# Attention with two half-array heads: where TensorE turns the values of the item before, and which engine divides them by their sums

## The chip, the cores and the metric

The kernel runs on one core of one Trainium2 chip. The metric is the device time of one execution in microseconds, the smaller the better. The core's engines are TensorE (PE in the profile, with its weight loads as PEld), VectorE (DVE), ScalarE (ACT), GpSimd (POOL) and SyncE (SP, which here only issues DMAs). They run their own instruction streams and meet at semaphores.

## The reference

The program is a sandwich of two layers over 4 x 2048 tokens of 256 channels: a recurrent scan, a routed feed-forward stage, a first attention with rotary embedding, and a second one with grouped projections. The change touches the first attention alone:

```python
# 16 heads of 16 channels; the batch is 4, the sequence is 2048 here
q = _apply_rope(xq, cos, sin)
k = _apply_rope(xk, cos, sin)
scores = jnp.einsum('bqhd,bkhd->bhqk', q, k) / jnp.sqrt(jnp.asarray(HEAD_DIM, dtype=q.dtype))
attn = jax.nn.softmax(scores, axis=-1)
out = jnp.einsum('bhqk,bkhd->bqhd', attn, xv)
```

## The kernel before

`phase_attention` (from L239) is called twice. With 16 channels a head (`DH = 16`) its flag `TWO` is true, and there are `N = 64` items, one for each pair of batch and head. With 32 channels a head `TWO` is false, and none of the touched code is used in that call.

An item is worked through in a window of `NSB = 64` steps. Every engine has its own list of what it does at each step, written out in Python (`window(n, s)`), unrolled for 12 items, then a loop of three rounds of 12 items, then the last 16 unrolled. What follows is the order within one window.

- **Scores and exponentials.** At each step TensorE makes one tile of 128 keys by 512 queries (`scores`, L550, tile `S`, written `at_S` in the profile). The contraction has 48 rows of split queries and keys and two rows with the running maximum, so 50 rows. At even steps it stands in rows 0 to 49 of the array, at odd steps in rows 64 to 113 (`HALVES`). ScalarE takes the exponential into `PB` (`exps`, L630). The tiles `S` are a ring of `NSR = 3` PSUM banks.
- **Maxima of the item after.** At each even step TensorE also makes two tiles of 512 scores (`max_scores`, L521, tile `MX`, 48 rows), one in rows 0 to 47 and one in rows 64 to 111. VectorE takes the negated maximum of both (`maxima`, L684). `MX` is a ring of two, so the matmuls of step t wait for the reduction of step t - 4. After 32 reductions a small one (L689) and a transpose (L540, step 50) give the rows of maxima of the next item; GpSimd splits them in two (`m_parts`, L456 and L458).
- **Values.** At each even step four products of 128 keys with a part of 256 queries (`values`, L561, tile `AV`) add up the numerators and, in one column, the sum. They are in fp32, so the profile counts eight matmuls. They use the full 128 rows and 32 of the array's columns each.
- **Turning.** The values of item n - 1 are complete after step 4 of window n. ScalarE copies `AV` to `AVS` after the exponential of step 4 (`put_values`, L638). TensorE turns `AVS` with four fp32 transposes of 128 x 128 (`turn_values`, L580) into a bank of the ring `S`. ScalarE copies this to `FO` (`take_values`, L648). Then VectorE takes the reciprocal of the 16 sums of each partition (`invert_turned`, L695), GpSimd multiplies (`normalise_turned`, L466) into `O`, and SyncE stores `O`.

`OUT_STEP` is 7. Before the change TensorE's order around it is: `MX` and `S` of step 6, the values of step 6 (the first of item n, which wait until `AVS` is copied), the four transposes, `S` of step 7, `MX` and `S` of step 8, the values of step 8. The list `places(n)` gives the ring `S` its order of occupants. ScalarE does `take_values` ahead of the exponential of step 7. VectorE and GpSimd do their parts at step 11.

Of the kernel before, what the change touches and what calls it, by code (L numbers as in the profile page):

```python
# [7 lines left out]
ALU = mybir.AluOpType  # L8
# [230 lines left out]
def phase_attention(nc, tag, H, DH, scale, qk_d, v_d, out_d, ident_d):  # L239
# [61 lines left out]
    def places(n):  # L301

        out = []
        for t in range(NSB):
            if TWO and t == OUT_STEP and (not isinstance(n, int) or n > 0):
                out.append(("out", 0))
            out.append(("score", t))
            if t == TURN_AT and later(n, 1):
                out.append(("turn", 0))
        return out  # L310
# [20 lines left out]
    with ExitStack() as ctx:  # L331
# [109 lines left out]
        @block.gpsimd  # L441
        def _(pool):
            for u in range(NBUF):
                for h in HALVES:
                    lo = (h + NQ) // 32 * 32
                    ins = nc.gpsimd.memset(KT[u][lo:lo + 32, :].bitcast(F32), 1.0)
                ins.then_inc(preset, 1)
            if not TWO:
                pool.wait_ge(preset, NBUF)
                nc.gpsimd.memset(ONES[:, :], 1.0).then_inc(preset, 1)  # L450

            def m_parts(it):

                wait(pool, mrow, 32 * len(HALVES) * it)
                wait(pool, nmf_got, it + 1, pool_step)
                nc.gpsimd.tensor_copy(NMR[:, 0, :], NMF[:, :]).then_inc(nmr_split, 1)  # L456
                wait(pool, nmr_split, it + 1)
                nc.gpsimd.tensor_tensor(NMR[:, 1, :], NMF[:, :], NMR[:, 0, :].bitcast(F32),  # L458
                                        ALU.subtract).then_inc(nmr_ready, 1)

            def normalise_turned(it, s):
                fo = FO[s % 2][:, :].rearrange("p (j c d) -> p j c d", j=W // P, c=NCH)
                out = O[s % 2][:, :, :].rearrange("p (c j) d -> p j c d", c=NCH)
                wait(pool, ostored[s % 2], 8 * NSTORE * it - 8 * NSTORE * (s % 2), pool_step)
                wait(pool, rec_done, it + 1, pool_step)
                nc.gpsimd.tensor_tensor(out, fo[:, :, :, 0:DH],  # L466
                                        REC[s % 2][:, :, :].to_broadcast([P, W // P, NCH, DH]),
                                        ALU.mult).then_inc(norm_done, 1)

            def add(it, i, kb):  # L470

                first = GROUPS[i][0]
                k = NCH * kb % NPB
                total = SUM[(len(GROUPS) * it + i) % 2]
                wait(pool, exp_done, NSB * it + NCH * (kb + 1))
                if kb == first + 1:
                    k0 = NCH * first % NPB
                    wait(pool, l_done, len(GROUPS) * it + i - 1)
                    other = PB[:, k0:k0 + NCH, :]
                else:  # L480
                    wait(pool, sum_done, NADD * it + added(kb) - 1)
                    other = total[:, :, :]
                nc.gpsimd.tensor_tensor(total[:, :, :], other, PB[:, k:k + NCH, :], ALU.add).then_inc(sum_done, 1)  # L483

            m_parts(0)

            def adds(n, s, t):
                for i, (a, b) in enumerate(GROUPS):
                    for kb in range(a + 1, b):
                        if NCH * (kb + 1) == t:  # L490
                            add(n, i, kb)

            def window(n, s):
                for t in range(NSB):
                    for unit in running(n, s, t):
                        adds(*unit)
                    if TWO and t == OUT_STEP + 4 and (not isinstance(n, int) or n > 0):
                        normalise_turned(n - 1, s + NBUF - 1)
                    if t == TURN_AT and later(n, 1):
                        m_parts(n + 1)  # L500
            rounds(pool, window)
            if TWO:
                normalise_turned(N - 1, N - 1)
            for t in range(NSB, 2 * NSB):
                adds(N - 1, N - 1, t)

        @block.tensor
        def _(pe):
# [90 lines left out]
            def window(n, s):  # L599

                for t in range(NSB):
                    tile = tile_at(t)
                    if TWO and t == OUT_STEP and (not isinstance(n, int) or n > 0):
                        slot_free(n, "out")
                        turn_values(n - 1, s + NBUF - 1, item(n, s, "out")[1])
                    if tile and later(n, tile[0]):
                        max_scores(n + tile[0], s + tile[0], tile[1])
                    scores(n, s, t)
                    for unit in running(n, s, t):
                        outputs(*unit)  # L610
                    if t == TURN_AT and later(n, 1):
                        slot_free(n, "turn")
                        max_turn(n + 1, item(n, s, "turn")[1])
# [7 lines left out]
        @block.scalar  # L621
        def _(act):
            def exps(it, s, t):
                old, of = (t - NPB, it) if t >= NPB else (t + (NSB - 1 - t) // NPB * NPB, it - 1)
                wait(act, av_done, NBLK * of + old // NCH + 1)
                if not TWO:
                    wait(act, sum_done, NADD * of + added(old // NCH))
                i, r = item(it, s, "score", t)
                wait(act, s_put, i + 1)
                nc.scalar.activation(PB[:, t % NPB, :], SP_[r][:, :],  # L630
                                     ACT.Exp, scale=scale).then_inc(exp_done, 1)

            def put_values(it, s):

                if not TWO:
                    wait(act, norm_done, it - 1)
                wait(act, av_done, NBLK * (it + 1))
                nc.scalar.activation(AVS[s % 2][:, :], AV[:, :], ACT.Copy).then_inc(avs_ready, 1)  # L638

            def take_turned(it, i, r):  # L640
                wait(act, nmr_ready, it)
                wait(act, s_put, i + 1)
                nc.scalar.activation(NMF[:, :], SP_[r][0:NBLK, 0:P], ACT.Copy).then_inc(nmf_got, 1)  # L643

            def take_values(it, s, i, r):
                wait(act, norm_done, it - 1)
                wait(act, s_put, i + 1)
                nc.scalar.activation(FO[s % 2][:, :], SP_[r][:, :], ACT.Copy).then_inc(fo_got, 1)  # L648

            def put_sums(it):  # L650

                wait(act, rec_done, NCH * it)
                wait(act, l_done, len(GROUPS) * (it + 1))
                nc.scalar.activation(LS[:, :], L[:, :], ACT.Copy).then_inc(ls_ready, 1)  # L654

            def window(n, s):
                for t in range(NSB):
                    if TWO and t == OUT_STEP and (not isinstance(n, int) or n > 0):
                        take_values(n - 1, s + NBUF - 1, *item(n, s, "out"))
                    exps(n, s, t)  # L660
                    for it, s_, t_ in running(n, s, t):
                        if END_STEP == t_:
                            put_values(it, s_)
                        if not TWO and sum_step(len(GROUPS) - 1) + 1 == t_:
                            put_sums(it)
                    if t == TURN_AT and later(n, 1):
                        take_turned(n + 1, *item(n, s, "turn"))
            take_turned(0, 0, 0)
            rounds(act, window)
            put_values(N - 1, N - 1)  # L670
            if TWO:
                take_values(N - 1, N - 1, TAIL, TAIL % NSR)
            else:
                put_sums(N - 1)

        @block.vector
        def _(dve):
# [10 lines left out]
                    wait(dve, nmf_got, it)  # L688
                    nc.vector.tensor_reduce(NM[:, :], NM4[:, :, :], AX_X, ALU.min).then_inc(nm_ready, 1)  # L689

            def invert_turned(it, s):
                fo = FO[s % 2][:, :].rearrange("p (j c d) -> p j c d", j=W // P, c=NCH)
                wait(dve, norm_done, it - 1)
                wait(dve, fo_got, it + 1)
                nc.vector.reciprocal(REC[s % 2][:, :, :], fo[:, :, :, DH]).then_inc(rec_done, 1)  # L695

            def invert(it, s, q):

# [25 lines left out]
            def window(n, s):  # L724
                for t in range(NSB):
# [4 lines left out]
                        for unit in running(n, s, t):  # L730
                            outputs(*unit)
                    if TWO and t == OUT_STEP + 4 and (not isinstance(n, int) or n > 0):
                        invert_turned(n - 1, s + NBUF - 1)
            rounds(dve, window)
            if TWO:
                invert_turned(N - 1, N - 1)
            else:
                for t in range(NSB, 2 * NSB):
                    outputs(N - 1, N - 1, t)
# [1172 lines left out]
```

## Time and profile before

| | us |
|---|---|
| median of 3 runs | 6774.84 |
| the three runs | 6770.58, 6774.84, 6792.63 |
| the profiled execution: its own time | 6770.58 |
| its span, first to last instruction | 6768.8 |
| the first attention, roughly | 1657 to 4340 of the span |

The profile is of one execution. "Busy" is time in which an engine had an instruction in work; the ends of matmuls are modelled, so their starts are what to read. An idle time is put down to what ended it. A row of the chronological view merges neighbours of a kind: "x4" are four instructions.

### The profile page before, as it was taken

What the parts mean: (1) busy time and instruction counts of PE and PEld (TensorE: products, weight loads), DVE (VectorE), ACT (ScalarE), POOL (GpSimd) and SP (SyncE); (2) the same over time, 40 slices, a digit from 0 to 9 for tenths busy, and PEclk for the clock granted to TensorE, in tenths of its full rate; (3) what the DMA queues carried; (4) which work ended last, traced back from release to release, by engine and by line L of the source; (5) the groups of instructions that cost most, each with busy time, mean ns of one, the idle gap of its engine ahead of it and who ended that gap; (6) DMA issues with size and microseconds to landing.
All of it is one profiled execution on the core that took longest, in us unless ns stands there. A gap on an engine that the chain in (4) does not pass through costs nothing. (4 is left out here: it accounts for less than half of the span.)

```text
span 6768.8 us, 116415 instructions
## 1 busy us (share of the span) xinstructions
PE 5861.4 (87%) x39184; PEld 2627.0 (39%) x39184; DVE 5338.4 (79%) x7223; ACT 4001.9 (59%) x7095; POOL 2223.9 (33%) x1114
## 2 busy tenths in 40 slices
PE   5996766675999999999999999756999999999992
PEld 3443541442333333333333333333444444444432
DVE  6996510775999999999999999587878787888855
ACT  3773101110788888888888888611556666666660
POOL 2332100343000000000000000011789888888891
PEclk9998866776999999999999999865999999999995
DMA  4112566455333333333333333286111111111106
GB/s 140 50 47 95 175 245 227 133 175 139 48 49 49 52 54 47 53 52 50 49 49 49 49 53 46 66 242 182 37 38 38 37 38 38 38 32 35 39 6 202
DMA packets 373239, 548.75 MB, mean 81 GB/s; under 512 B 68464, under 2 KB 273200, under 8 KB 352976
## 3 DMA queue, kind: packets, MB, share of 16 engines
q1 hardware_dynamic: 359888, 524.77, 32.1%
q10 hardware_dynamic: 12800, 16.78, 0.7%
q8 instruction: 328, 5.37, 0.3%
q14 instruction: 223, 1.83, 0.1%
HBM read 352.02 MB, written 186.78 MB: 80 GB/s over the span
## 5 line engine op out<-in xcount | busy, mean ns | idle before, releaser
L684 DVE TENSOR_REDUCE at_NM<-at_MX 128x1 f32<-128x1024 f32 (+1 forms) x4096 | 3750.4, 950 | 550.7 <-PE at_MX L521 517.3
L630 ACT ACTIVATE at_PB<-at_S 128x512 f32<-128x512 f32 x6144 | 3308.1, 599 | 977.0 <-PE at_S L550 859.7
L521 PE MATMUL at_MX<-at_KT,at_QT 48*128 48x512 f32 (+1 forms) x6144 | 2408.3, 454 | 169.5 <-DVE at_NM L684 91.0
L550 PE MATMUL at_S<-at_QT,at_KT 50*128 50x512 f32 (+1 forms) x6144 | 2339.1, 435 | 6.7 <-ACT at_PB L630 3.8
L561 PE MATMUL at_AV<-at_PB,at_VS 128*32 128x256 f32 (+1 forms) x20480 | 1821.4, 437 | 18.5 <-ACT at_AVS L638 13.2
L550 PEld LDWEIGHTS at_S<-at_QT,at_KT 50*128 50x128 f32 (+1 forms) x6144 | 1009.9, 188 | 904.0 <-issue 477.8
L521 PEld LDWEIGHTS at_MX<-at_KT,at_QT 48*128 48x128 f32 (+1 forms) x6144 | 996.7, 190 | 738.4 <-DVE at_NM L684 555.7
L483 POOL TENSOR_TENSOR at_SUM<-at_SUM,at_PB 128x2048 f32<-128x2048 f32 x192 | 885.2, 4610 | 60.8 <-ACT at_PB L630 44.7
L561 PEld LDWEIGHTS at_AV<-at_PB,at_VS 128*32 128x32 f32 x20480 | 431.5, 108 | 1018.6 <-ACT at_PB L630 784.6
L483 POOL TENSOR_TENSOR at_SUM<-at_PB 128x2048 f32<-128x2048 f32 x160 | 749.9, 4688 | 148.8 <-ACT at_PB L630 148.3
L456 POOL CAST at_NMR<-at_NMF 16x128 fp32r<-16x128 f32 x96 | 26.9, 280 | 1630.3 <-ACT at_NMF L643 1630.3
L1354 ACT ACTIVATE r_XT<-r_PT 128x1024 f32<-128x1024 f32 x48 | 49.2, 1024 | 569.8 <-PE r_PT L1263 569.8
L466 POOL TENSOR_TENSOR at_O<-at_FO,at_REC 128x256 f32<-128x256 f32 x64 | 39.8, 622 | 1027.0 <-DVE at_REC L695 1027.0
L833 PE MATMUL wkv_PQ<-wkv_XT,wkv_WT 128*128 128x512 f32 x768 | 339.2, 598 | 42.6 <-DVE wkv_DL L953 25.8
L833 PEld LDWEIGHTS wkv_PQ<-wkv_XT,wkv_WT 128*128 128x128 f32 x768 | 144.1, 191 | 237.3 <-issue 192.9
L1204 POOL TENSOR_SCALAR r_veps<-r_mv 128x4 f32<-128x4 f32 x112 | 25.7, 229 | 601.9 <-DVE r_mv L1414 601.9
L912 POOL TENSOR_TENSOR wkv_EV<-wkv_E2S,wkv_V 128x1024 f32<-128x1024 f32 x32 | 75.6, 2362 | 355.0 <-DVE wkv_MN L931 152.9
L1250 PE MATMUL r_PA<-r_OW,r_A 128*128 128x256 f32 x512 | 137.0, 434 | 62.9 <-DVE r_X L1478 47.8
L572 PE MATMUL at_L<-at_SUM,at_ONES 128*32 128x512 f32 x1280 | 177.3, 627 | 8.0 <-POOL at_SUM L483 8.0
L703 DVE RECIPROCAL at_REC<-at_LS 128x128 f32<-128x128 f32 x128 | 119.8, 940 | 71.9 <-ACT at_LS L654 71.9
L1283 PE MATMUL r_QK<-r_WQ,r_XT 128*128 128x512 f32 x256 | 153.4, 732 | 19.8 <-ACT r_XT L1354 19.8
L1434 DVE TENSOR_TENSOR r_RT<-r_QK,r_ROPE 128x256 f32<-128x256 f32 x256 | 90.2, 414 | 89.8 <-PE r_QK L1283 87.0
(153 smaller groups left out, 4181.1 us busy)
## 6 DMA issues: line engine op xcount, KB each, us to landing
moe_W<-in_w SPq DMA_DIRECT2D x64, 1024.0 KB, 10.8
at_QT<-qk SPq DMA_DIRECT2D x384, 128.0 KB, 5.9
at_KT<-qk SPq DMA_DIRECT2D x384, 128.0 KB, 7.3
qk<-r_HI SPq DMA_DIRECT2D x64, 512.0 KB, 4.1
qk<-r_LO SPq DMA_DIRECT2D x64, 512.0 KB, 4.7
x<-r_X SPq DMA_DIRECT2D x48, 512.0 KB, 3.0
at_VS<-v SPq DMA_DIRECT2D x96, 256.0 KB, 8.5
at_QT<-qk SPq DMA_DIRECT2D x96, 256.0 KB, 4.1
```

Source lines behind the costliest of these rows:

```text
L483: nc.gpsimd.tensor_tensor(total[:, :, :], other, PB[:, k:k + NCH, :], ALU.add).then_inc(sum_done, 1)
L521: ins = nc.tensor.matmul(MX[r][:, a, :], QT[u][h:h + NQ, b * P:(b + 1) * P], KT[u][h:h + NQ, (c + a) * W:(c + a + 1) * W], start=True, sto ...
L550: nc.tensor.matmul(SP_[item(it, s, "score", t)[1]][:, :], KT[u][h:h + NQ + 2, kb * P:(kb + 1) * P], QT[u][h:h + NQ + 2, c * W:(c + 1) * W] ...
L561: ins = nc.tensor.matmul(AV[c * VW:(c + 1) * VW, cols], VS[s % NBUF][:, kb, :], PB[:, (NCH * kb + c) % NPB, cols], start=first, stop=last)
L572: ins = nc.tensor.matmul(L[c * VW:(c + 1) * VW, :], ONES[:, :], SUM[(len(GROUPS) * it + i) % 2][:, c, :], start=(i == 0), stop=(i == len(G ...
L630: nc.scalar.activation(PB[:, t % NPB, :], SP_[r][:, :], ACT.Exp, scale=scale).then_inc(exp_done, 1)
L684: nc.vector.tensor_reduce(NM4[:, b, c:c + 1], MX[r][:, :, :].rearrange("p a n -> p (a n)"), AX_X, ALU.max, negate=True).then_inc(ring_got, 1)
L703: nc.vector.reciprocal(REC[s % 2][:, part], LS[:, part]).then_inc(rec_done, 1)
L833: ins = nc.tensor.matmul(PQ[q][:, tt * 512:(tt + 1) * 512], WT[:, cc, row:row + P], XT[b % 2][:, cc, t0:t0 + 512], start=(cc == 0), stop=( ...
L1250: ins = nc.tensor.matmul(PA[:, j, :], A[u][:, q, t], OW[:, q, :], start=(q == 0), stop=(q == 2 * CC - 1))
L1283: ins = nc.tensor.matmul(QK[j % 2][:, :], XT[u][:, c, t], WQ[:, c, 0:2 * D], start=(c == 0), stop=(c == CC - 1))
L1434: ins = nc.vector.tensor_tensor(RT[k][:, :, :, :], qk[:, :, :, :, r], cs[f][:, :, :, :], ALU.mult)
```

## The change

Two things are done together, both only for `TWO`.

1. In step 7 the turning comes behind the score tile, on TensorE (the score matmul is issued first and then the four transposes), on ScalarE (the exponential first, then the copy to `FO`) and in the list of places of the ring.
2. GpSimd's `normalise_turned` is taken out. VectorE's `invert_turned` becomes `normalise_turned`: it takes the reciprocal, waits for its own result (`rec_done`) and for the earlier store of `O` (`ostored`), and multiplies itself. Its old wait for `norm_done` goes.

```diff
         for t in range(NSB):
+            out.append(("score", t))
             if TWO and t == OUT_STEP and (not isinstance(n, int) or n > 0):
                 out.append(("out", 0))
-            out.append(("score", t))
...
-            def normalise_turned(it, s):
-                fo = FO[s % 2][:, :].rearrange("p (j c d) -> p j c d", j=W // P, c=NCH)
-                out = O[s % 2][:, :, :].rearrange("p (c j) d -> p j c d", c=NCH)
-                wait(pool, ostored[s % 2], 8 * NSTORE * it - 8 * NSTORE * (s % 2), pool_step)
-                wait(pool, rec_done, it + 1, pool_step)
-                nc.gpsimd.tensor_tensor(out, fo[:, :, :, 0:DH],
-                                        REC[s % 2][:, :, :].to_broadcast([P, W // P, NCH, DH]),
-                                        ALU.mult).then_inc(norm_done, 1)
-
...
                     tile = tile_at(t)
-                    if TWO and t == OUT_STEP and (not isinstance(n, int) or n > 0):
-                        slot_free(n, "out")
-                        turn_values(n - 1, s + NBUF - 1, item(n, s, "out")[1])
                     if tile and later(n, tile[0]):
                         max_scores(n + tile[0], s + tile[0], tile[1])
                     scores(n, s, t)
                     for unit in running(n, s, t):
                         outputs(*unit)
+                    if TWO and t == OUT_STEP and (not isinstance(n, int) or n > 0):
+                        slot_free(n, "out")
+                        turn_values(n - 1, s + NBUF - 1, item(n, s, "out")[1])
...
-                    if TWO and t == OUT_STEP and (not isinstance(n, int) or n > 0):
-                        take_values(n - 1, s + NBUF - 1, *item(n, s, "out"))
                     exps(n, s, t)
...
+                    if TWO and t == OUT_STEP and (not isinstance(n, int) or n > 0):
+                        take_values(n - 1, s + NBUF - 1, *item(n, s, "out"))
...
-            def invert_turned(it, s):
+            def normalise_turned(it, s):
                 fo = FO[s % 2][:, :].rearrange("p (j c d) -> p j c d", j=W // P, c=NCH)
-                wait(dve, norm_done, it - 1)
+                out = O[s % 2][:, :, :].rearrange("p (c j) d -> p j c d", c=NCH)
                 wait(dve, fo_got, it + 1)
                 nc.vector.reciprocal(REC[s % 2][:, :, :], fo[:, :, :, DH]).then_inc(rec_done, 1)
+                wait(dve, rec_done, it + 1)
+                wait(dve, ostored[s % 2], 8 * NSTORE * it - 8 * NSTORE * (s % 2))
+                nc.vector.tensor_tensor(out, fo[:, :, :, 0:DH],
+                                        REC[s % 2][:, :, :].to_broadcast([P, W // P, NCH, DH]),
+                                        ALU.mult).then_inc(norm_done, 1)
```

## Rows read from the trace of the kernel before

**Rows 1.** The page, the span in 40 equal slices: busy tenths, granted TensorE clock.

```profile
PE   5996766675999999999999999756999999999992
DVE  6996510775999999999999999587878787888855
ACT  3773101110788888888888888611556666666660
PEclk9998866776999999999999999865999999999995
```

**Rows 2.** Two stretches of 400 us inside the first attention, busy time by engine.

```profile
1800.00:2200.00 400.00, 397.60 (x3818) 149.98 (x3814) 384.47 (x334) 350.99 (x657) 12.87 (x29) 1.00 0.33 49
3400.00:3800.00 400.00, 397.69 (x3816) 150.15 (x3809) 383.31 (x334) 351.17 (x657) 12.76 (x28) 1.00 0.35 52
```

**Rows 3.** ScalarE's copy to FO, between 2900 and 3100 us.

```profile
L648 ACT ACTIVATE at_FO<-at_S x5: 598/598/598, 2906.8 to 3069.9; 128x512 f32<-128x512 f32 x5
```

**Rows 4.** Who TensorE waited for between 1800 and 4300 us.

```profile
PE at_AV L561 <- ACT at_AVS L638: 12.2, 58, 0.5
PE at_MX L521 <- issue: 6.3, 4, 2.9
PE at_AV L561 <- issue: 5.2, 2, 2.9
```

**Rows 5.** TensorE in order of time, steps 5 to 8 of one window.

```profile
2904.65 0.50 PE L550 MATMUL at_S<-at_QT,at_KT 50*128 50x512 f32 x1
2904.66 0.73 PE L521 MATMUL at_MX<-at_KT,at_QT 48*128 48x512 f32 x2
2905.00 0.40 PE L550 MATMUL at_S<-at_QT,at_KT 50*128 50x512 f32 x1
2905.58 0.64 PE L561 MATMUL at_AV<-at_PB,at_VS 128*32 128x256 f32 x8 [0.18 <-ACT at_AVS L638]
2906.15 0.66 PE L580 MATMUL at_S<-at_ident,at_AVS 128*128 128x128 f32 x4
2906.73 0.49 PE L550 MATMUL at_S<-at_QT,at_KT 50*128 50x512 f32 x1
2906.74 0.72 PE L521 MATMUL at_MX<-at_KT,at_QT 48*128 48x512 f32 x2
2907.07 0.40 PE L550 MATMUL at_S<-at_QT,at_KT 50*128 50x512 f32 x1
2907.40 0.64 PE L561 MATMUL at_AV<-at_PB,at_VS 128*32 128x256 f32 x8
```

**Rows 6.** TensorE at the last item, where no MX matmuls are left.

```profile
4333.05 0.50 PE L550 MATMUL at_S<-at_QT,at_KT 50*128 50x512 f32 x1
4333.48 0.42 PE L561 MATMUL at_AV<-at_PB,at_VS 128*32 128x256 f32 x4
```

**Rows 7.** TensorE in the second attention, matmuls of one kind in a row.

```profile
5501.82 0.40 PE L550 MATMUL at_S<-at_QT,at_KT 98*128 98x512 f32 x1
5502.06 0.40 PE L521 MATMUL at_MX<-at_KT,at_QT 96*128 96x512 f32 x1
```

**Rows 8.** ScalarE in order of time, steps 5 to 12 of the same window as rows 5.

```profile
2906.84 0.60 ACT L648 ACTIVATE at_FO<-at_S 128x512 f32<-128x512 f32 x1 [0.34 <-PE at_S L580]
2907.33 3.49 ACT L630 ACTIVATE at_PB<-at_S 128x512 f32<-128x512 f32 x6
```

**Rows 9.** VectorE in order of time, the same window, and TensorE's MX of step 16.

```profile
2909.88 0.25 DVE L695 RECIPROCAL at_REC<-at_FO 128x16 f32<-128x16 f32 x1
2910.04 1.16 DVE L684 TENSOR_REDUCE at_NM<-at_MX 128x1 f32<-128x1024 f32 x1
2911.69 0.50 PE L521 MATMUL at_MX<-at_KT,at_QT 48*128 48x512 f32 x1
```

**Rows 10.** Start of the phase, where MX waits for VectorE, in order of time.

```profile
1656.95 2.35 DVE L684 TENSOR_REDUCE at_NM<-at_MX 128x1 f32<-128x1024 f32 x2 [53.56 <-PE at_MX L521]
1659.36 0.80 PE L521 MATMUL at_MX<-at_KT,at_QT 48*128 48x512 f32 x2 [0.33 <-DVE at_NM L684]
```

**Rows 11.** VectorE in order of time, later in the same window.

```profile
2927.34 1.23 DVE L684 TENSOR_REDUCE at_NM<-at_MX 128x1 f32<-128x1024 f32 x1
2928.60 0.19 DVE L689 TENSOR_REDUCE at_NM<-at_NM 128x16 f32<-128x32 f32 x1
2928.91 5.86 DVE L684 TENSOR_REDUCE at_NM<-at_MX 128x1 f32<-128x1024 f32 x5
```

**Rows 12.** Multiplications on VectorE: one line each, shortest/median/longest in ns.

```profile
L1434 DVE TENSOR_TENSOR r_RT<-r_QK,r_ROPE x256: 389/414/426, 1212.9 to 1600.7; 128x256 f32<-128x256 f32 x128
L709 DVE TENSOR_TENSOR at_O<-at_AVS,at_REC x32: 691/3854/4160, 4830.5 to 6612.6; 128x512 f32<-128x512 f32 x32
```

**Rows 13.** The end of the first attention, in order of time.

```profile
4337.60 0.26 DVE L695 RECIPROCAL at_REC<-at_FO 128x16 f32<-128x16 f32 x1 [34.81 <-ACT at_FO L648]
4338.00 0.62 POOL L466 TENSOR_TENSOR at_O<-at_FO,at_REC 128x256 f32<-128x256 f32 x1 [34.44 <-DVE at_REC L695]
```

More of the change, by code:

```diff
@@ L496, in window @@
                         adds(*unit)
-                    if TWO and t == OUT_STEP + 4 and (not isinstance(n, int) or n > 0):
-                        normalise_turned(n - 1, s + NBUF - 1)
                     if t == TURN_AT and later(n, 1):
@@ L501, in _ @@
             rounds(pool, window)
-            if TWO:
-                normalise_turned(N - 1, N - 1)
             for t in range(NSB, 2 * NSB):
@@ L732, in window @@
                     if TWO and t == OUT_STEP + 4 and (not isinstance(n, int) or n > 0):
-                        invert_turned(n - 1, s + NBUF - 1)
+                        normalise_turned(n - 1, s + NBUF - 1)
             rounds(dve, window)
             if TWO:
-                invert_turned(N - 1, N - 1)
+                normalise_turned(N - 1, N - 1)
             else:
```

## The prediction

> **What bounds the kernel now.** I read the slices first [rows 1]: the first attention is the long stretch (about 1657 to 4340 us) in which TensorE and VectorE both stand at 9 and ScalarE at 8, with the clock at full speed. Busy shares can't say which of the two sets the pace (TensorE 398 of 400 us, VectorE 384 [rows 2]), so I went on to the waits. TensorE has three entries between 1800 and 4300 us [rows 4]: its values waiting for the copy to AVS (12.2 us in 58 windows, 0.2 each), and two for "issue". It never waits for VectorE's reductions nor for an exponential. An engine that waits for nobody sets the pace. One window takes (3069.9 - 2906.8) / 4 = 40.8 us [rows 3].
>
> Then the starts on TensorE, around the turning [rows 5]. Two steps are a packet: S and MX start together (2904.65, 2904.66), then MX and S (2905.00), then the eight of AV. From the four transposes on, the distances are: transposes to the next packet 0.58, first pair to second pair 0.34, second pair to AV 0.33, and AV to AV over the whole piece 1.82, of which 1.24 are a normal packet (0.34 + 0.33, and 0.57 for AV: 2906.15 - 2905.58). So the turning costs 0.58 us of TensorE's time, and whatever is added to TensorE here is added to the window.
>
> **The change on TensorE.** Nothing is added to the list, only an order is changed: S of step 7 goes ahead of the transposes. But S of step 7 loses its partner. Before, S(7) stood in the rows from 64 on and the first MX in rows 0 to 47, and they started together; then the second MX (64 on) and S(8) (0 on). After it, S(7) runs alone between AV and the transposes, the two MX start together, and S(8) stands alone behind them. Three rounds instead of two.
>
> What the additional round costs: at the last item there is an S all alone, cold, with a matmul of another kind behind it: 4333.05 to 4333.48, 0.43 us [rows 6]. It is the same situation (S first after AV, then a matmul that uses the array otherwise). The rest keeps its distances: AV to S(7) as AV to the transposes before, transposes to the MX pair 0.58, MX pair to S(8) 0.34, S(8) to AV 0.33 [rows 5]. New path less old path: (0.43 + 0.58 + 0.34 + 0.33) - (0.58 + 0.34 + 0.33) = **0.43 us for each window**. From below it is bounded by 0.24 us, the distance at which full-height matmuls of one kind follow each other with their weights loaded ahead [rows 7]; and by 0, if TensorE had slack after all. From above I take 0.53: the MX pair is now cold (0.50 long against 0.40 for a second one [rows 5]), if S(8) pays for that as well. I take 0.43, since the row is the very pair of neighbours.
>
> The Trainium skill (TensorEngine Tiling (Array Packing), Key Properties) says that a change of tiling mode, not of tile, drains the array. The order before has two changes between AV and S(7); the new one has three up to MX. The trace agrees that such a border costs something: 0.33 from a second pair to AV against 0.24 within one kind [rows 5, 7]. By the border alone, 0.09 us a window, the sum below would be 62 x 0.09 = 6 us.
>
> Windows 1 to 63 turn a value. The last has no MX and waits for its exponentials, so 62 count: 62 x 0.43 = **+26.7 us**.
>
> **ScalarE.** It is idle 0.34 us ahead of the copy to FO [rows 8], as it waits for the transposes with nothing to do. With S(7) first it has an exponential for this time. The idle goes, and is worth nothing: behind the copy come six exponentials without a gap in 3.49 us, ScalarE catches up, and TensorE waits for none of them [rows 4]. The wait for AVS stays too, since both orders have the values of step 6 ahead. New in the ring: S(10) now follows FO. The copy ends some 0.43 us later than now, at 2906.84 + 0.60 = 2907.44 [rows 8], and S(10) starts 0.57 + 0.34 behind the AV of 2907.40, at 2908.31 [rows 5], and also comes 0.43 later, which leaves some 0.8 us. No price.
>
> **VectorE.** It gets the multiplication, 128 x 256. Nearest row: 414 ns at that shape [rows 12]. L709 has both inputs in SBUF as this one: 691 ns at 512 columns at its shortest, so 414 at 256 fits; the upper bound is that 691. L709's median of 3854 ns is under GpSimd's long additions in the second attention; in the first, GpSimd works 13 us in 400 [rows 2], and nothing at step 11.
>
> The Trainium skill (SBUF — State Buffer, Who interferes with whom) says a VectorE instruction with two SBUF inputs and a GpSimd one that reads SBUF block each other. The trace agrees by that spread of 691 to 4160 ns; a lock of this sort would cost 3 us a window, and has no partner here.
>
> Does it reach TensorE? VectorE has time over: behind the small reduction it runs five large ones at (5.86 - 1.22) / 4 = 1.16 us [rows 11] where a packet gives it 1.24. But the ring of two MX is short. The reduction of step 12 ends at 2910.04 + 1.16 = 2911.20, and MX(16) starts at 2911.69, 0.49 later [rows 9]. Where MX does wait for VectorE, it starts 0.06 behind the reduction's end (1656.95 + 2.35 = 1659.30, then 1659.36) [rows 10]. So VectorE may come 0.43 us later than now. After the change, behind the reciprocal come 0.25 for its end, a wait for its own result (0.03 to 0.04, as the small reduction starts behind the large one's end, 2928.57 [rows 11]; up to 0.15, as GpSimd takes 0.14 with the same two waits [rows 13]), 0.41 for the multiplication, less 0.08 of overlap: the reduction starts 0.62 to 0.73 behind the reciprocal's start, not 0.16 [rows 9]. That is 0.46 to 0.57 later, against 0.43 to spare. TensorE stalls 0.03 to 0.14 us; I take 0.07, nearer the lower end, as it is VectorE's own row (up to 0.35 with a multiplication of 691 ns; 0 from below), once, since VectorE gains 0.08 on each further packet. 62 x 0.07 = **+4.3 us**. What hides the remaining 0.4 us is the slack of the ring; without it the multiplication would cost 62 x 0.5 = 31 us.
>
> **GpSimd and SyncE.** GpSimd loses 622 ns a window of work nobody waited for; its maxima at step 50 come at the same time. `norm_done` comes earlier, so the store does. Only at the end of the phase it counts: reciprocal to end of product is 1.02 us now [rows 13], and 0.25 + 0.04 + 0.41 = 0.70 after: -0.3 us, once.
>
> **Sum.** +26.7 + 4.3 - 0.3 = +30.7 us. On the profiled execution's own 6770.6 us that is 6801; the median of the runs is 4.3 us higher, 6775, which gives 6806. I give 6804, +0.45%.
>
> **The rivals.** A measurement of this kernel can't tell less than about 0.3%, 20 us, from no change.
>
> *The product is dear.* At 691 ns or with slow waits the stall is 0.35 us a window: 62 x 0.35 = 22 in place of 4, in all 6822. For it speaks the odd access pattern (a broadcast input, an output in another order), against it that no row in this kernel shows a pattern to matter.
>
> *The lone S is cheap.* It costs only the border between kinds (0.09) or the bare stream of its columns (0.24 [rows 7]): 6 to 15 us over 62 windows; with 2 us of stall 6779 to 6788 on the own time. For it: 0.43 holds 0.10 of weight load, which might overlap the AV before. Against: S after AV always shows 0.50.
>
> *Nothing on the path.* If VectorE or ScalarE had set the pace all along, the lone S would be hidden: 6771 to 6777. Against it, TensorE's empty list of waits.
>
> *Faster: ScalarE's gap was the path.* If the stream of exponentials decides the window, the 0.34 us ahead of FO fall out: 62 x 0.34 = 21 us, 6751. For it: ScalarE idles there in every window. It decides from the point where a score tile or value waits for an exponential at steps 8 to 12, and none does.
>
> **How the numbers follow.** Forecast 0.56 (6793 to 6813 by itself), dear product 0.14, cheap S 0.13, nothing 0.09, faster 0.08. Leaving out the faster case and the dearest end gives a range of 6776 to 6819. Slower by over 0.3%: the forecast less its lowest end, and the dear product, 0.66. Within 0.3%: 0.26. Faster: 0.08.
>
> **What would show it.** In the profile after: copies to FO 41.3 us apart, not 40.8. On TensorE after AV(6) an S alone, transposes 0.43 later, two MX starting together, an S 0.34 behind. AV(6) to AV(8) 2.25 us, not 1.82. On ScalarE no idle ahead of FO. On VectorE the product 0.41 long, some 0.04 to 0.15 behind the reciprocal, and the reduction 0.6 to 0.7 behind its start. A first wait of MX for a reduction on TensorE's list, near step 16, under 0.15 us each. It is wrong if the transposes follow S(7) in 0.25 or less, or if TensorE's gap at step 16 is above 0.3.

## The result: 0.7% slower, beyond the range

| | median us | runs |
|---|---|---|
| before | 6774.84 | 5 (6770.58 to 6792.63) |
| changed | 6836.81 | 5 (6822.44 to 6839.26) |
| ratio over all runs of the comparison | 1.007 | 95% interval 1.0057 to 1.0083 |

I had forecast 6804 with a range of 6776 to 6819 and slower at 0.66. The direction held, the size did not: +62 us between the first medians, where I had +31 to the own time. Those two medians are an unlucky pair, one below and the other above the mean of its kernel. Over 17 runs the changed kernel took 6828.7 us in the mean, and the kernel before 6780.6 over 5 here and 6782 to 6787 in three later comparisons (19 to 24 runs each). The first comparison gives +48 us, a later one +45, and all runs on record together (22 and 71) +45. I go on with **+47 us**, of which my steps give two thirds.

The profiled execution took 6836.09 us (span 6834.3). The slices of the page that answer to [rows 1]:

```profile
PE   5996766775999999999999999765999999999993
DVE  6996510775999998998999999587878788878855
ACT  3773101111888888888888888611466666656660
PEclk9998866776999999999999999865899999999995
```

Inside the first attention nothing is to be seen at this grain but an 8 twice in VectorE's row, where it had only 9. The two places matter later.

ScalarE's copy to FO, unrolled windows first, then windows of the loop (answer to [rows 3]; before it was 40.8 in both):

```profile
L635 ACT ACTIVATE at_FO<-at_S x4: 597/598/598, 1929.4 to 2053.4; 128x512 f32<-128x512 f32 x4
...
L635 ACT ACTIVATE at_FO<-at_S x4: 597/597/597, 2982.7 to 3106.8; 128x512 f32<-128x512 f32 x4
```

That is 124.0 / 3 = 41.33 and 124.1 / 3 = 41.37 us a window. TensorE in order of time at steps 6 to 8 of a loop window, the answer to [rows 5]:

```profile
2980.98 0.64 PE L548 MATMUL at_AV<-at_PB,at_VS 128*32 128x256 f32 x8 [0.18 <-ACT at_AVS L625]
2981.55 0.50 PE L537 MATMUL at_S<-at_QT,at_KT 50*128 50x512 f32 x1
2981.98 0.66 PE L567 MATMUL at_S<-at_ident,at_AVS 128*128 128x128 f32 x4
2982.57 0.50 PE L508 MATMUL at_MX<-at_KT,at_QT 48*128 48x512 f32 x2
2982.91 0.40 PE L537 MATMUL at_S<-at_QT,at_KT 50*128 50x512 f32 x1
2983.23 0.64 PE L548 MATMUL at_AV<-at_PB,at_VS 128*32 128x256 f32 x8
```

S(7) stands alone; the transposes start 0.43 behind it, the two MX together 0.59 further on, S(8) 0.34 behind them, AV 0.32 behind that. AV to AV is 2.25 us, before 1.82.

The lone S pays for a round of its own between two borders, and not for its missing partner as such. In the last windows of the kernel before, two score matmuls in the two halves stand between the transposes and the values, and they take the same 0.43:

```profile
4301.68 0.50 PE L550 MATMUL at_S<-at_QT,at_KT 50*128 50x512 f32 x2
4302.11 0.42 PE L561 MATMUL at_AV<-at_PB,at_VS 128*32 128x256 f32 x4
```

VectorE in order of time in the same window, and TensorE at step 16 (answer to [rows 9]):

```profile
2985.71 0.24 DVE L682 RECIPROCAL at_REC<-at_FO 128x16 f32<-128x16 f32 x1
2986.08 0.43 DVE L685 TENSOR_TENSOR at_O<-at_FO,at_REC 128x256 f32<-128x256 f32 x1
2986.42 2.35 DVE L671 TENSOR_REDUCE at_NM<-at_MX 128x1 f32<-128x1024 f32 x2
...
2987.52 0.50 PE L537 MATMUL at_S<-at_QT,at_KT 50*128 50x512 f32 x1
2987.70 0.56 PE L508 MATMUL at_MX<-at_KT,at_QT 48*128 48x512 f32 x2
```

The same places in an unrolled window:

```profile
2015.02 0.24 DVE L682 RECIPROCAL at_REC<-at_FO 128x16 f32<-128x16 f32 x1
2015.30 0.43 DVE L685 TENSOR_TENSOR at_O<-at_FO,at_REC 128x256 f32<-128x256 f32 x1
2015.64 1.22 DVE L671 TENSOR_REDUCE at_NM<-at_MX 128x1 f32<-128x1024 f32 x1
...
2016.84 0.50 PE L537 MATMUL at_S<-at_QT,at_KT 50*128 50x512 f32 x1
2016.91 0.66 PE L508 MATMUL at_MX<-at_KT,at_QT 48*128 48x512 f32 x2
```

S and MX of step 16 used to start together. Now MX comes 0.18 later in the loop (0.16 of it reach the window) and 0.07 later unrolled, since the product starts 0.13 behind the end of the reciprocal in the loop (2985.95 to 2986.08) and 0.04 behind it unrolled. In the unrolled code the values it waits for are constants, in the loop they depend on the round; that this makes the difference is likely, and was not tested. In the unrolled window MX starts 0.05 behind the end of the reduction (2016.86), the same distance as in [rows 10], so it is the reduction that it waits for, although TensorE's list of waits has no entry of that name. The two stalls and the lone S are the whole change in an ordinary window: 0.43 + 0.07 = 0.50 and 0.43 + 0.16 = 0.59. Over 26 unrolled and 36 loop windows that is 34.2 us; with the 0.60 by which the loop's windows differ over the whole trace it is 34.6. I go on with **34.5 us**. Some 12 of the 47 us are not in ordinary windows.

They are in the first attention all the same. From the first copy to FO to the last it takes 2582.4 us before and 2634.5 after, 52 more; in the second traces of the two kernels, taken later, it takes 2586.1 and 2630.6, 44 more. So 10 to 18 us of the phase are beyond its windows:

```profile
L648 ACT ACTIVATE at_FO<-at_S x64: 597/598/600, 1754.5 to 4336.9; 128x512 f32<-128x512 f32 x64
L635 ACT ACTIVATE at_FO<-at_S x64: 592/597/598, 1763.8 to 4398.3; 128x512 f32<-128x512 f32 x64
```

These are behind the loop's back edges, the two places where the loop jumps back to its head. Two stretches of each trace, around the first and the second back edge; the columns are as in [rows 2] (busy time of TensorE, its weight loads, VectorE, ScalarE and GpSimd, then the granted clock, the DMA share and GB/s). Before, and after:

```profile
2690.00:2790.00 100.00, 95.70 (x881) 35.94 (x881) 87.88 (x77) 81.02 (x152) 3.31 (x7) 0.95 0.35 51
3180.00:3290.00 110.00, 104.55 (x964) 39.16 (x964) 96.53 (x85) 89.09 (x167) 3.32 (x7) 0.95 0.34 50
```

```profile
2690.00:2790.00 100.00, 94.64 (x756) 34.52 (x754) 76.36 (x69) 70.18 (x130) 1.45 (x4) 0.81 0.28 42
3180.00:3290.00 110.00, 103.90 (x864) 38.20 (x863) 87.66 (x78) 80.52 (x150) 1.45 (x4) 0.86 0.27 41
```

The clock has two levels, 2.4 and 1.2 GHz, so a mean of 0.95 over 100 us are 10 us at the lower one, and 0.81 are 38. At each back edge TensorE stands still twice for some 3 us, and from the second stop on the clock is at half. The first back edge of the kernel before, and behind it the values of a packet every 2.16 us:

```profile
2691.08 0.51 PE L521 MATMUL at_MX<-at_KT,at_QT 48*128 48x512 f32 x2 [2.92 <-issue]
2694.74 1.08 PE L561 MATMUL at_AV<-at_PB,at_VS 128*32 128x256 f32 x8 [2.86 <-issue]
2696.89 1.08 PE L561 MATMUL at_AV<-at_PB,at_VS 128*32 128x256 f32 x8
2699.05 1.08 PE L561 MATMUL at_AV<-at_PB,at_VS 128*32 128x256 f32 x8
```

The stops are the second and third line of [rows 4], which the prediction left out of its sum. In the kernel before the clock stayed at half for 10 and 11 us, in the changed one for 38 and 31. TensorE stays "busy" in both, at half the pace (756 matmul records in place of 881), so busy time doesn't show it. The Trainium skill (Runtime: NRT & Kernel Launch, Instruction fetch mechanics) says that a taken branch can force a fetch of instructions by DMA before execution goes on. The trace agrees with that: the stops stand at the loop's back edges, and nowhere in the phase when it is written out, and in the 10 us around the two stops (2685 to 2695) nine packets of the kind "instruction" land, where 40 us of straight code (2720 to 2760) have seven.

```profile
q8 instruction: 3, 0.05, 2.4%
q14 instruction: 6, 0.05, 1.6%
```

### The profile page after: what moved, and what is told of

The parts are those of the page before. It is cut to its first block and busy times, and to the rows that moved or that the text cites. A ratio compares the mean times of both kernels' runs of the same rounds, so it can differ in the third digit from the quotient of the medians.

```text
span 6834.3 us, 116275 instructions
## 1 busy us (share of the span) xinstructions
PE 5932.6 (87%) x39184; PEld 2657.6 (39%) x39184; DVE 5352.9 (78%) x7287; ACT 4013.1 (59%) x7095; POOL 2186.3 (32%) x1050
## 3 DMA queue, kind: packets, MB, share of 16 engines
q14 instruction: 222, 1.82, 0.1%
## 5 line engine op out<-in xcount | busy, mean ns | idle before, releaser
L537 PE MATMUL at_S<-at_QT,at_KT 50*128 50x512 f32 (+1 forms) x6144 | 2369.2, 437 | 6.7 <-ACT at_PB L617 3.7
L537 PEld LDWEIGHTS at_S<-at_QT,at_KT 50*128 50x128 f32 (+1 forms) x6144 | 1024.1, 189 | 930.7 <-issue 506.6
L1242 PEld LDWEIGHTS r_PA<-r_OW,r_A 128*128 128x128 f32 x512 | 112.5, 223 | 95.2 <-issue 68.7
```

Of the source, the lines that this page charges most:

```text
L537: nc.tensor.matmul(SP_[item(it, s, "score", t)[1]][:, :], KT[u][h:h + NQ + 2, kb * P:(kb + 1) * P], QT[u][h:h + NQ + 2, c * W:(c + 1) * W] ...
L1242: ins = nc.tensor.matmul(PA[:, j, :], A[u][:, q, t], OW[:, q, :], start=(q == 0), stop=(q == 2 * CC - 1))
```

## The experiments

Three theories on the 12 us: the order makes the half-clock stretches longer (A), the product on VectorE does (B), their length is chance and the same in both kernels (C).

**Part 1 alone** (the order of places, of TensorE and of ScalarE, without the product; of its edit only the list of places is shown):

```diff
+            out.append(("score", t))
             if TWO and t == OUT_STEP and (not isinstance(n, int) or n > 0):
                 out.append(("out", 0))
-            out.append(("score", t))
...
```

> Part 1 alone: the turning behind the score of step 7, the product stays on GpSimd. Both theories: TensorE pays 0.43 us a window for the lone score matmul, windows of 41.2 us in place of 40.8, +27 us over 62. They differ on the half-clock stretches behind the two back edges of the loop, which were 10 us long each before and 38 and 31 us after. Theory A (the order makes them long): again some 30 us or more, about +20 us on top, +45 in all. Theory B (the product on VectorE makes them long): 10 us, +27 in all. Theory C (their length is set by where the back edge falls in time, whatever the kernel): anything between, and the kernel before shows long ones too in some executions.

Measured: 1.0064 (1.0041 to 1.0087), +39 us in the mean of 4 runs (error 7), where its windows give 27. ScalarE's copy to FO in the loop:

```profile
L648 ACT ACTIVATE at_FO<-at_S x6: 597/597/597, 2920.5 to 3126.4; 128x512 f32<-128x512 f32 x6
```

205.9 / 5 = 41.18 us, 0.42 above before. By the granted clock (0.95 of 100 us, 0.83 of 110) the stretches were 10 and 37 us: one as before, one long.

**Part 2 alone** (the product on VectorE, the old order; GpSimd's multiplication is gone as in the change):

```diff
+                wait(dve, rec_done, it + 1)
+                wait(dve, ostored[s % 2], 8 * NSTORE * it - 8 * NSTORE * (s % 2))
+                nc.vector.tensor_tensor(out, fo[:, :, :, 0:DH],
+                                        REC[s % 2][:, :, :].to_broadcast([P, W // P, NCH, DH]),
+                                        ALU.mult).then_inc(norm_done, 1)
```

> Part 2 alone: the product on VectorE, the turning ahead of the score of step 7 as before. MX of step 16 waits for VectorE: 0.07 us in an unrolled window, 0.16 in a window of the loop, 27 x 0.07 + 35 x 0.16 = +7.5 us; no lone score, so the pairs stay. Theory A: the half-clock stretches stay at 10 us, +7.5 in all. Theory B: they are 30 us or more, +27. Theory C: either.

Measured: 1.0016 (1.0004 to 1.0028), +9 us in the mean of 10 runs, where its windows give 7.5. Stretches of 18 and 11 us (0.91 and 0.95). Theory B's +27 did not come. The two parts, +0.64% and +0.16%, add up to 0.80%, and both together took 0.70% and 0.71%; the intervals cover the difference.

**The kernel before once more.**

> The kernel before, unchanged, once more with a profile: windows of 40.8 us. Theories A and B: half-clock stretches of 10 us behind the back edges and 6771 to 6775 us. Theory C: in some executions 20 to 40 us and 6790 us, as two of the five timed runs of before.

6775.4 us, one run. The same two stretches of the trace:

```profile
2690.00:2790.00 100.00, 94.74 (x817) 34.88 (x817) 82.11 (x72) 75.60 (x141) 2.69 (x6) 0.88 0.28 42
3180.00:3290.00 110.00, 104.36 (x975) 39.07 (x973) 97.36 (x86) 89.93 (x170) 3.42 (x8) 0.97 0.28 43
```

24 and 7 us: the length is not a constant of the kernel. The trace that I predicted from had two short ones.

**The turning behind the score of step 8**, product on GpSimd. It tests the account of pairs and borders: this place is no earlier than the changed one, but breaks no pair and adds no border. The reciprocal and the product stay at step 11.

```diff
-    OUT_STEP = END_STEP + 3 - NSB
+    OUT_STEP = END_STEP + 4 - NSB
...
                     scores(n, s, t)
+                    if TWO and t == OUT_STEP and (not isinstance(n, int) or n > 0):
+                        slot_free(n, "out")
+                        turn_values(n - 1, s + NBUF - 1, item(n, s, "out")[1])
                     for unit in running(n, s, t):
                         outputs(*unit)
```

> The turning behind the score of step 8 and ahead of the values of step 8, so that no pair of score and MX is broken and there is no further border between kinds; the product stays on GpSimd. By the account of pairs and borders it costs TensorE nothing: windows of 40.8 us, +0 us. If it was the later turning itself that cost (a bank of the ring of scores that comes free later, a later copy to FO), it costs as much as part 1 or more: 41.2 us and +27. Theory A, taken as the broken pair: stretches of 10 us.

Measured: 0.9986 (0.9973 to 0.9999). TensorE in order of time:

```profile
2952.24 0.49 PE L550 MATMUL at_S<-at_QT,at_KT 50*128 50x512 f32 x1
2952.24 0.72 PE L521 MATMUL at_MX<-at_KT,at_QT 48*128 48x512 f32 x2
2952.58 0.40 PE L550 MATMUL at_S<-at_QT,at_KT 50*128 50x512 f32 x1
2952.90 0.66 PE L580 MATMUL at_S<-at_ident,at_AVS 128*128 128x128 f32 x4
2953.49 0.64 PE L561 MATMUL at_AV<-at_PB,at_VS 128*32 128x256 f32 x8
```

The pairs are whole, S to the transposes is 0.32 (not 0.43), the transposes to AV 0.59, and the window does not grow. What cost in the change is the round that the lone S has to itself, not the later turning. The missing partner and the additional border come together in part 1, and no run parts them. Stretches of 10 and 13 us.

**Part 1 only at the head of each round** (windows 12, 24, 36), **and everywhere but there.** A function of the place in the code picks the order; in the loop `s` runs from 0 to 11 in every round:

```diff
+    def behind(s):
+        return TWO and (s in (0, 12, 24, 36))
...
-                    if TWO and t == OUT_STEP and (not isinstance(n, int) or n > 0):
+                    if not behind(s) and TWO and t == OUT_STEP and (not isinstance(n, int) or n > 0):
```

> Part 1 only in the windows 12, 24 and 36 (those at the head of a round of the loop; 24 and 36 come behind a back edge), all other windows as before. The lone score matmul costs 3 x 0.43 = 1.3 us. Theory A (a lone score matmul at step 7 behind a back edge keeps the clock down longer): +12 us or more in the mean, stretches of 30 us. Theory C (the length is chance, alike in both kernels): +1 us.

Measured: 1.0009 (0.9997 to 1.0021), +5 us in the mean of 11 runs, stretches of 10 and 31 us. It lies between theory C's +1 and A's +12, with an error of 4, and so decides nothing.

The other kernel has `s not in (0, 1, 48)`:

> Part 1 in all windows but 1, 12, 24, 36 and 48, which keep the old order: 58 or so windows at 0.43 us are +25 us. Theory A: that and no more, since behind the back edges nothing is changed. Theory C: the same +25. If part 1 costs more than its windows wherever it stands: +35.

Since `s` is 1 in the loop too, the windows 13, 25 and 37 kept the old order as well, and 54 windows pay and not 58: 23 us. Measured: 1.0032 (1.0021 to 1.0044), +21 us in the mean of 6 runs. Nothing on top, as A says; stretches of 28 and 18 us. With this one and the last, neither the heads of the rounds alone nor the other windows alone show the 12 us, so they can't be pinned on the windows right behind an edge.

**The changed kernel once more.**

> The changed kernel once more, on the chip of the other three. Its windows cost 27 x 0.50 + 35 x 0.60 = +34.5 us. Theory A: +47 with longer stretches in most executions. Theory C: +35 in the mean over many runs, and the +62 between the first medians was partly luck.

Measured: 1.0071 (1.0058 to 1.0085), +45 us in the mean, with an error of 3. Stretches of 28 and 37 us (0.86 of 100, 0.83 of 110). The first ratio was no accident, and C's +35 is out.

**The turning behind step 8 once more.**

> The turning behind the score of step 8 once more, product on GpSimd, for a narrower interval: unrolled windows of 40.64 us in place of 40.83 and loop windows of 40.74 in place of 40.76, -5 us, so a ratio of 0.9992. The first comparison had 0.9986, a part of which would be chance.

Measured: 1.001 (1.0000 to 1.0021), where the first time it was 0.9986. The two intervals don't meet, so 0.1% between such sets of runs means nothing; with the loop this order is no faster. The two traces of this one kernel differ in their windows too: in the loop 40.75 us here, and there 40.48 and 40.74 in turn. Stretches of 24 and 7 us.

**Rounds of 4 items** (`UNR = 4`), to have 13 back edges in place of 2, for all four combinations.

> The kernel before with rounds of 4 items in place of 12 (UNR = 4), so 13 back edges in place of 2: each costs two stops of TensorE of some 3 us and a half-clock stretch, in all 9.4 us at the 10 us stretches of the first trace, so 11 more of them are +103 us or more, some 6885. It gives 13 stretches for the comparison with the next three. Theory C (length is chance): a mean of about 15 us, as in the five traces without a lone score matmul behind the edge, with single ones of 25 or 30.

> The changed kernel with rounds of 4 items. Against the kernel before with rounds of 4, the windows cost 62 x 0.43 and 56 x 0.16, +36 us. Theory A (lone score matmul behind an edge) or B (product): stretches of some 33 us in the mean in place of 15, 13 x 18 us at half clock, of which some 0.42 is lost, +98 us on top. Theory C: the same lengths as in the kernel before and +36 us.

> Part 1 alone with rounds of 4 items. Windows +27 us against the kernel before with rounds of 4. Theory A: most of the 98 us of longer stretches are here. Theory B: none of them, +27. Theory C: +27.

> Part 2 alone with rounds of 4 items. Windows +9 us against the kernel before with rounds of 4. Theory A: +9 and short stretches. Theory B: the long stretches are here, +100. Theory C: +9.

The stretch from 1900 to 4200 us, in the order before, changed, part 1 alone, part 2 alone:

```profile
1900.00:4200.00 2300.00, 2242.41 (x20481) 836.95 (x20478) 2059.66 (x1790) 1889.91 (x3528) 70.84 (x158) 0.95 0.32 47
```

```profile
1900.00:4200.00 2300.00, 2258.75 (x19897) 845.19 (x19899) 2011.32 (x1790) 1847.00 (x3427) 37.35 (x102) 0.92 0.32 46
```

```profile
1900.00:4200.00 2300.00, 2258.62 (x19969) 838.32 (x19967) 2009.70 (x1746) 1851.43 (x3438) 68.75 (x153) 0.92 0.32 47
```

```profile
1900.00:4200.00 2300.00, 2249.82 (x20385) 845.40 (x20381) 2057.00 (x1835) 1880.57 (x3510) 38.53 (x106) 0.95 0.32 47
```

A clock of 0.95 is 230 us at half clock, 0.92 is 368. It goes with the order, not with the product, so B is out. But the timed runs don't follow: 6949.6, 6989.4, 6982.5 and 6938.4 us in the mean of 5, 4, 4 and 4. Both kernels with the new order together are 42 us above both with the old one; their windows explain 27, so 13 back edges cost 15 us more, with an error of about 8, and not the 98 that I had expected of A. The profiled executions were the fastest of their kernel in the old order (6919.57, 6923.9) and among the slowest in the new (7000.95), so the traces overstate it. Part 2 alone came out 11 us below before, where +9 had been expected; the error of that difference is 9. What these runs do show well: with rounds of 4 a back edge costs (6949.6 - 6782.3) / 11 = 15 us on average, and the 9.4 us in the trace of before was a cheap one.

**The 64 windows written out** (`UNR = N`), so that there is no back edge at all.

> The kernel before with the first attention's 64 windows all written out (no loop, so no back edge). All theories: windows of 40.83 us, no stop of 3 us on TensorE and no half-clock stretch inside the phase. 35 windows at +0.07 are +2 us; two back edges gone are -19 us by the first trace of before, -30 us by the 15 us that each further edge cost in the runs with rounds of 4. So -17 to -28 us, a ratio of 0.996 to 0.9975.

> The changed kernel with the 64 windows written out. Against the one before written out: 62 x 0.50 = +31 us by the windows. Theory A (the part of some 11 us that the windows leave unexplained is in the half-clock stretches behind the back edges): +31 and no more. If it is elsewhere (start of the phase, second attention, ends): +42.

Measured: the kernel before written out 0.9962 (0.995 to 0.9975), mean of 10 runs 6763.2; the changed one written out 1.0007 (0.9997 to 1.0017), mean of 12 runs 6788.3. Windows from 2900 us on, before and changed:

```profile
L648 ACT ACTIVATE at_FO<-at_S x5: 598/598/598, 2924.3 to 3087.6; 128x512 f32<-128x512 f32 x5
```

```profile
L635 ACT ACTIVATE at_FO<-at_S x5: 598/598/598, 2915.4 to 3080.5; 128x512 f32<-128x512 f32 x5
```

163.3 / 4 = 40.83 and 165.1 / 4 = 41.28 us. The second has one short window in it; nearly all others take 41.3, which is the 0.50 more. From the first copy to FO to the last it is 2564.2 and 2595.6 us, 31 more, as the windows say. The only wait left on TensorE in the phase is the one for AVS, the clock is 1.00 throughout, and the difference of the means is 25 us with an error of 3. The 12 us on top are gone with the back edges.

**The clock of the timed runs.** A trace shows one execution, but the mean granted clock of every timed run is on record too. Twice what is missing to 1, times the run's span, is its time at half clock, all phases together. The clock is given to three decimals, 14 us of this time, so only means say something:

| | us at half clock | runs |
|---|---|---|
| before, four comparisons | 1262 (error 3) | 71 |
| changed, two | 1287 (4) | 22 |
| part 1 alone | 1286 (8) | 4 |
| part 2 alone | 1262 (5) | 10 |
| part 1 at the heads alone, everywhere but there | 1269 (8), 1264 (5) | 11, 6 |
| turning behind step 8, first and second time | 1256 (4), 1283 (7) | 10, 12 |
| rounds of 4: old order, new order | 1521 (13), 1594 (14) | 9, 8 |
| written out: before, changed | 1237 (7), 1225 (3) | 10, 12 |

The changed kernel spends 24 us more at half clock, with an error of 5. A packet takes 2.16 us there for 1.24, so 0.43 of this time is lost: 10 us of the 12. Part 1 alone has the same 24, part 2 alone has none, so B is out in the timed runs as well, and C, which has the same lengths in both kernels, does not fit. Written out, the changed kernel has 12 us less at half clock than before and not more, worth 5 us, about as much as 25 falls short of the windows' 31. With rounds of 4 the new order has 73 us more, worth 31 (error 8), where the times left 15 (error 8). Two rows follow no simple rule: part 1 at the heads alone has no clear excess, and the turning behind step 8 has 1283 in its second set without any lone score.

**The turning behind step 8, written out**, the version that beats both.

> The turning behind the score of step 8, product on GpSimd, windows written out: unrolled windows of this order took 40.64 to 40.81 us against 40.83, so -1 to -12 us against the kernel before written out, with nothing from back edges to blur it.

Measured: 0.9954 (0.994 to 0.9968), 6752.65 us median of 6 runs. Of the 0.46%, 0.38% are the missing back edges; against the kernel before written out the means differ by 11 us, with an error of 3.

```profile
L648 ACT ACTIVATE at_FO<-at_S x7: 603/603/605, 2905.6 to 3149.4; 128x512 f32<-128x512 f32 x7
```

243.8 / 6 = 40.63 us a window. Behind the turning a packet takes 1.23 us in place of 1.24 in many windows; why was not tried.

## Why the prediction was right or wrong

- **What sets the pace.** Right. In an ordinary window TensorE waits for nobody but AVS before, and both what the order and what the late MX put on it are in the window.
- **The lone score, 0.43 us.** Right to the hundredth (0.43 in the trace, 0.42 by the windows of part 1 alone), because the row of the last item was the same pair of neighbours. The bounds of 0 and 0.24 were not needed. That the order costs, and not the later turning, is shown by the turning behind step 8: no earlier, no pair broken, no cost.
- **ScalarE's idle time.** Right that removing it is worth nothing. The idle ahead of FO is gone, and the rival that went faster with it.
- **The product on VectorE.** The mechanism right, to the step at which MX first waits. The wait for its own result is 0.04 unrolled and 0.13 in the loop; I had both as ends of a range and took a stall of 0.07 for all windows. Measured are stalls of 0.07 and 0.16, 7.5 us in place of 4.3. The sign that I had named for it, an entry on TensorE's list of waits, did not come; the starts show it. The product takes 0.43 us, not 0.69: the dear product did not come.
- **The sum.** Here it failed. It took the phase for 62 equal windows at full clock. "Issue" had a place in the list of waits [rows 4], 11.5 us, and the prediction put it at nothing and called the list empty: two stops of 3 us at each back edge, followed by a stretch at half clock. The term missing from the sum is the part of the cost that is paid behind the back edges, some 12 us. That it is there is shown by difference: 47 us less 34.5 with the loop, 25 against 31 without it. That most of it is a longer stay at half clock is what the clock of the timed runs says (24 us more, worth 10), and the profiles too. Over the ten traces with two back edges, the stretches with no lone S behind the edge average 15 us (twelve of them, 7 to 28), those with one 28 us (eight, 10 to 38); 13 us more cost 5.5, twice. Part 2 alone doesn't have it.
- **The range.** Its upper end came from one dear instruction. It should have held what varies from run to run: medians of before lie between 6774.8 and 6785.7 us, and I started from a trace with two short stretches. From a typical 6783 the same sum gives 6814, inside the range; the first median of the changed kernel is then 23 us off. Of the 33 us between 6804 and 6836.81, some 12 are the missing term, 3 the stall, 9 the level of before and 8 the luck of the changed kernel's first five runs; with average luck it would have been 6829, still outside. Much of what varies lies ahead of the phase: the first copy to FO starts at 1754.5 us in the trace of before and at 1781.8 in that of before written out.

Open: how the new order at step 7 keeps the clock down longer behind an edge, why the heads of the rounds alone don't show it clearly, and why 13 back edges show so little of it in the timed runs (15 us with an error of 8, 31 by their clock).

## What to carry to other kernels

Where matmuls use half of the array's rows, the order of the list decides which of them run together: moving one of them alone across another kind cost a full round here (0.43 us), although no work was added, and the place between two kinds that existed already cost nothing. An entry called "issue" on the engine that sets the pace is a term of the sum: look at what comes behind it, and compare the granted clock of the same stretch in two traces, since a TensorE at half clock looks as busy as ever. Where the clock of every timed run is on record, it tells more than one trace. And take the level of a kernel from many runs before adding to it; one trace may hold the cheap case of everything that varies.

## What the runs showed of the hardware

- A score matmul of 50 rows alone between two other kinds holds TensorE for 0.43 us, and so do two in the two halves; two pairs, one behind the other, take 0.34 and 0.33.
- VectorE starts 0.04 us behind the end of its own result in unrolled code, where the values waited for are constants, and 0.13 behind it in a loop, where they depend on the round.
- One back edge of this loop costs two stops of 2 to 3 us on TensorE and 7 to 38 us at half clock. In the kernel before that is 12 us of time on average with rounds of 12 windows (6785.7 - 6763.2 us and 2.4 for the windows, over two edges) and 15 with rounds of 4. Writing out the 64 windows saves 0.38%.
